# ScalarE stacks the row maxima itself, and the second scores follow 12 heads behind

## The reference, cut to what matters

```
x = x + attention0(layernorm(x), ctx, ctx)          # 16 heads of 16, no weights, softmax over 256 keys
x = x + moe(layernorm(x))                           # 64 experts, 8 of them for each token
x = x + attention1(layernorm(x), ctx) @ Wo.T        # projected q, k, v; causal
x = x + ffn(layernorm(x))                           # 16 blocks, 4 of them open for each token

scores = einsum('bqhd,bkhd->bhqk', q, k) * scale
attn   = softmax(scores)                            # exp(s - max over the keys) / sum
out    = einsum('bhqk,bkhd->bqhd', attn, v)
```

## Time and profile before

| | us |
|---|---|
| median of 3 runs | 1179.89 (1178.31 to 1189.08) |
| profiled execution, its own time | 1183.53 |
| its span | 1181.7 |
| busy: PE 934.0, PEld 627.6, DVE 614.7, ACT 360.8, POOL 535.2 | |
| DMA | 160.39 MB, mean 136 GB/s |

### The profile page before, as it was taken

The page is one execution under the profiler, slowest core; times in us unless marked ns, Lnnn a source line. Parts: engine busy times, 40 slices in busy tenths (PEclk is TensorE's granted clock), DMA queues, the critical chain, the costliest instruction groups (busy, mean ns, idle before and its releaser), DMA issues. The chain is left out here.

```text
span 1181.7 us, 22184 instructions
## 1 busy us (share of the span) xinstructions
PE 934.0 (79%) x5670; PEld 627.6 (53%) x5671; DVE 614.7 (52%) x1818; ACT 360.8 (31%) x884; POOL 535.2 (45%) x514
## 2 busy tenths in 40 slices
PE   1178778765499999999899999803788886799999
PEld 1035454454266666666666666502566664465665
DVE  6568988874144444444444444436878772333230
ACT  3426555613122222222222222111255564122211
POOL 4400776776476677676677667413253200000000
PEclk9999888988699999999999999955799999699999
DMA  6464534015455565555656666252877541100000
GB/s 221 156 161 126 112 87 101 24 32 170 139 188 187 160 206 186 179 183 176 194 186 207 206 199 205 78 218 70 251 193 213 147 105 30 58 9 10 18 18 19
DMA packets 78846, 160.39 MB, mean 136 GB/s; under 512 B 18448, under 2 KB 44048, under 8 KB 76480
## 3 DMA queue, kind: packets, MB, share of 16 engines
q1 hardware_dynamic: 59264, 112.23, 32.3%
q0 software_dynamic: 19520, 47.41, 13.0%
HBM read 118.09 MB, written 41.22 MB: 135 GB/s over the span
## 5 line engine op out<-in xcount | busy, mean ns | idle before, releaser
L1279 PE MATMUL ex_ps<-ex_w_gu,ex_rows_t 128*128 x640 | 263.1, 493 | 27.5 <-issue 17.0
L1248 POOL DMA_INDIRECT expert_outs<-ex_result,slot_places x160 | 157.4, 984 | 102.5 <-DVE ex_result L1391 101.6
L1243 POOL DMA_INDIRECT ex_rows<-moe_rows,slot_tokens x160 | 153.9, 962 | 57.7 <-issue 48.8
L881 POOL DMA_INDIRECT expert_lists<-rt_number,rt_idx x128 | 123.9, 968 | 105.8 <-DVE rt_idx L988 63.7
L1298 PE MATMUL ex_ps<-ex_w_down,ex_hidden_t 96*128 x640 | 166.8, 382 | 1.0 <-DVE ex_hidden_t L1383 1.0
L616 ACT ACTIVATE a_probs<-a_ps 128x512 f32<-128x512 f32 (+1 forms) x256 | 133.2, 541 | 96.3 <-PE a_ps L478 48.1
L1353 ACT ACTIVATE ex_act_g<-ex_ps 128x192 f32<-128x192 f32 x160 | 52.9, 330 | 353.3 <-PE ex_ps L1279 353.3
L461 PE MATMUL a_ps<-stacked_keys,a_qst 96*128 96x256 bf16 (+1 forms) x512 | 109.6, 287 | 56.4 <-DMA stacked_keys<-k_stack 26.7
L1279 PEld LDWEIGHTS ex_ps<-ex_w_gu,ex_rows_t 128*128 128x128 f32 x640 | 108.4, 192 | 43.2 <-issue 36.0
L1391 DVE TENSOR_SCALAR ex_result<-ex_ps,ex_rows 128x256 f32<-128x256 f32 x160 | 77.4, 484 | 93.5 <-PE ex_ps L1298 93.5
L1298 PEld LDWEIGHTS ex_ps<-ex_w_down,ex_hidden_t 96*128 96x128 f32 x640 | 108.3, 189 | 13.1 <-issue 2.4
(11 more groups left out here) (222 smaller groups left out, 1408.7 us busy)
## 6 DMA issues: line engine op xcount, KB each, us to landing
ex_w_gu<-in_w_gu_dram SPq DMA_DIRECT2D x64, 384.0 KB, 3.3
cb_gathered<-expert_outs SPq DMA_DIRECT2D x16, 1024.0 KB, 5.6
ex_w_down<-in_w_down_dram SPq DMA_DIRECT2D x64, 192.0 KB, 3.9
a_qst<-q_stack SPq DMA_DIRECT2D x32, 192.0 KB, 4.0
stacked_keys<-k_stack SPq DMA_DIRECT2D x32, 192.0 KB, 4.1
a_qst<-q_stack SPq DMA_DIRECT2D x32, 128.0 KB, 3.8
stacked_keys<-k_stack SPq DMA_DIRECT2D x32, 128.0 KB, 4.0
k_stack<-split_parts SPq DMA_DIRECT2D x8, 384.0 KB, 2.6
```

The source lines that it names most:

```text
L881: nc.gpsimd.indirect_dma_start(k.lists, bass.IndirectOffsetOnAxis(ap=self.idx[:, t, s:s + 1], axis=0), self.number[:, t, s:s + 1], None).t ...
L1243: nc.gpsimd.indirect_dma_start(rows[:, t % R, :], None, k.xn.rearrange("t p d -> (t p) d"), bass.IndirectOffsetOnAxis(ap=k.ids[:, begin + ...
L1248: nc.gpsimd.indirect_dma_start(k.outs, bass.IndirectOffsetOnAxis(ap=k.places[:, begin + t:begin + t + 1], axis=0), result[:, t % R], None) ...
L1279: last = pe.matmul(ps[:, 2 + j % 2, 0:2 * FF], rows_t[:, j % 2, c * P:(c + 1) * P], w_gu[:, bass.ds(ring, 1), c, :].rearrange("p a n -> p ...
```

## The change

In the first attention (`causal` false) and there alone:

- `qst` and the rows of `kst` that are used grow from 98 to 112. Rows 96 to 111 of the queries hold all 16 maxima rows (2 parts for each of 8 heads), the same in each head's slot; in the keys' stack, in head s's slot, rows 96+s and 104+s are ones and the other fourteen zeros.
- ACT writes these rows straight from PSUM into `qst` (`place_maxima`), in two copies of four heads' slots, 16x1024 each, at s = 1 and s = 2. `maxrows`, its copy and SP's two DMAs for each step are gone. `max_copied` counts both copies.
- POOL fills the one-hot rows at the start of the block with four `tensor_tensor` of 16x2048, ahead of its routing work. The fill with ones, which stood in `prepare`, now stands at the start of the second attention's block, ahead of `Combine`'s sums.
- `second(st, s)` puts the second scores, and all that hangs on them, 12 heads behind; the turn of the maxima moves from s = 4 to s = 1; `START` goes from 6 to 2.

```diff
-START = 6
+START = 2
...
+        def second(st, s):
+
+            at = s + (0 if causal else 4)
+            return (after(st, -LAG), at) if at < HSTEP else (after(st, 1 - LAG), at - HSTEP)
...
+                if causal:
+                    nc.gpsimd.memset(kst[ROWS:ROWS + mrows], 1.0).then_inc(keys_marked, 4)
+                    pool.wait_ge(keys_marked, 4)
+                else:
+                    heads = [k.ident_b[ROWS:ROWS + mrows, ROWS + part * HSTEP:ROWS + (part + 1) * HSTEP].unsqueeze(2).to_broadcast([mrows, HSTEP, SEQ])
+                             for part in range(2)]
+                    for u in range(4):
+                        nc.gpsimd.tensor_tensor(kst[ROWS:ROWS + mrows, u], heads[0], heads[1], ALU.add).then_inc(keys_marked, 1)
+                        pool.wait_ge(keys_marked, u + 1)
...
+                    if not causal and s % 4 == 0:
+                        pe.wait_ge(max_copied, 2 * h + 1 + s // 4)
...
-                        pe.wait_ge(max_copied, min(h + LAG, STEPS) if isinstance(h, int) else h + LAG)
+                        copies = 1 if causal else 2
+                        pe.wait_ge(max_copied, copies * min(h + LAG, STEPS) if isinstance(h, int) else copies * h + copies * LAG)
...
+                def place_maxima(st, g):
+                    h, u = number(st), st[1]
+                    act.wait_ge(max_turned, h + 1)
+                    nc.scalar.copy(qst[ROWS:ROWS + mrows, u, 4 * g:4 * g + 4, :],
+                                   max_t.unsqueeze(1).to_broadcast([mrows, 4, SEQ])).then_inc(max_copied, 1)
```

51 lines of the change are left out of this document (27 added, 24 removed).

## The result

| | before | changed |
|---|---|---|
| median, compared together (4 runs each) | 1184.49 us | 1197.30 us (1196.00 to 1202.48) |
| ratio, 95% interval | | 1.012 (1.0065 to 1.0175) |
| profiled execution, its span | 1183.53, 1181.7 us | 1196.41, 1194.5 us |
| mean granted clock of TensorE | 0.930 | 0.924 |

The change makes the kernel about 1.2% slower. The forecast was 1182.5 us, within 1175 to 1190: wrong. Of the 14.8 us between the forecast and 1197.3 us, 4.6 lie in the starting point (the forecast stood on a median of 1179.9 us of three runs, which with the fourth is 1184.5); the rest is the change, +12.8 us where +2.6 was forecast. The span grew by 12.8 us, and the block that was changed accounts for it: the scatter's last issue moved by 14.65 us.

A forecast was written before the change was run, and what follows sets the result against it. GpSimd's last scatter was taken to bound the kernel. Ramp -3.4, longer steps +2.4 and +2.0, then the sixth element's later places put its last issue at 295.3, +2.6 us: 1179.9 + 2.6 = 1182.5 us, range 1175 to 1190.

The forecast's parts named there:

- What bounds: First attention's block: GpSimd's last scatter ends it, at 292.72 us, and the kernel's time moves by as much.
- The ramp: Start of the attention: second scores at 72.7 us, the fifth head's 3.4 us earlier, bounds 0 to 3.7.
- The held cut: VectorE's two cuts at the start, beside GpSimd's additions: first held until 69.3 us, second slips through, 0 us in sum.
- the rival: Start of the attention: second cut held until 73.9 us, 2.8 us on top of the forecast, +5.4 in all; chance 0.10.
- Each step gets longer: Attention loop: outputs wait for ScalarE's copies; 0.6 us for each of four steps (+2.4), 0.25 for each of eight (+2.0).
- PE drops to half clock: Attention loop: PE's waits lower its granted clock; all five intervals at 23.3 us give +5.7 us; chance 0.12.
- near half clock: Attention loop wholly at half clock: an element takes 26.8 us, +23 us; chance 0.04.
- The sixth element binds: Scatter: sixth element's places come 21.9 us after the fifth's, at 231.1 us, so the last issue is at 295.3 us.
- the stall of the scatter: GpSimd's scatter: one stall of 4.2 us kept in the sum; a rival had it gone, 4.2 less, chance 0.05.
- Parts at nothing: Moved fill with ones (covered by 5.5 us in the second attention), SP's dropped DMAs and 112-row contraction: 0 us.

The follow-up runs named there:

- e14: Kernel with 12 heads' distance and DMA'd maxima (e2), order of the first scores' banks shifted by five heads: 1191.4 us, ratio 1.0042 to the kernel before.
- e1: Changed kernel with second scores 16 heads behind again and START 6, maxima still copied by ScalarE: 1185.8 us, ratio 1.0001 to the kernel before.
- e9: Kernel with 12 heads' distance and DMA'd maxima (e2), order of the first scores' banks shifted by four heads: 1189.3 us, ratio 1.0043 to the kernel before.
- e12: Kernel with 12 heads' distance and DMA'd maxima (e2), plus 12 useless transposes at head 7 of each step: 1190.0 us, ratio 1.0034 to the kernel before.
- e15: Changed kernel with only the filling added, the turn at head 7 done seven times over: 1200.2 us, ratio 1.0110 to the kernel before.
- e8: Kernel before with only the order of the first scores' three banks shifted by four heads: 1199.6 us, ratio 1.0130 to the kernel before.
- e2: Changed kernel with 12 heads kept, but maxima moved by one ScalarE copy and two DMAs as before: 1199.6 us, ratio 1.0134 to the kernel before.
- e16: e14 with the filling added, the turn at head 7 done seven times over: 1192.7 us, ratio 1.0065 to the kernel before.
- e17: e13 with head 7's second scores computed five times over in each step: 1196.1 us, ratio 1.0082 to the kernel before.
- e13: Kernel before with the order of the first scores' banks shifted by one head: 1183.0 us, ratio 0.9996 to the kernel before.
- e18: Changed kernel with banks shifted by five heads, first four heads' outputs one head later, and the filling at head 7: 1204.2 us, ratio 1.0149 to the kernel before.

## Why the prediction was wrong

- **What bounds: right.** The last scatter sets the end; it moved 14.65 us, the profiled execution 12.9; the difference was made up behind it.
- **The ramp: right in sign, too small.** Second scores at 71.23 us (forecast 72.7), fifth head's 5.3 us earlier (3.4). ScalarE's copies took 1.00 us (1.05), GpSimd's additions 3.60 us (4.5), and 1.7 us of the gain is the earlier load of step 1, which was not in the sum. (In the working of the copy, 1.55 us for 1792 numbers is 0.89 us for 1024, not 0.86; the sum does not use it.)
- **The held cut: right that it costs nothing, in part by luck.** The additions were shorter than forecast and ended at 68.79 us, not 73.9. The first cut was held, for 2.37 us, but by the fourth addition and not by the third. When the second cut came no addition was left to hold it, so the rival's +2.8 us had lost its condition, and this trace does not decide between the forecast and the rival. The Trainium skill, "GPSIMD Engine Reference", "Key points", names contention for VectorE's instructions with two SBUF inputs, and the second cut has two; no run here has it beside an addition. The held operations, this cut and the one in the earlier trace rows, have one SBUF input; whether they use both ports no row shows. That an operation with two SBUF inputs can slip through is shown elsewhere, in the second attention of the kernel before, where L87 starts between two of GpSimd's instructions, one that began at 800.91 us and took 4.49 us, and the next at 805.48 us:

```profile
801.08 4.34 DVE L85 SCALAR_TENSOR_TENSOR cb_newton<-cb_rstd 128x2 f32<-128x2 f32 x1
805.46 0.16 DVE L87 SCALAR_TENSOR_TENSOR cb_newton<-cb_moments,cb_newton 128x2 f32<-128x2 f32 x1
805.48 2.34 POOL L1504 TENSOR_TENSOR cb_gathered<-cb_gathered 128x1024 f32<-128x1024 f32 x1
```
- **"Each step gets longer": this step failed.** I took 0.6 us for each of the four steps before the first places and 0.25 us for each of the next eight. Measured: (119.31 - 118.72 + 5.3) / 4 = 1.47 us and (99.22 - 89.49) / 8 = 1.22 us. The mechanism that I put there is real (18 waits of 1.7 us; VectorE waited 12.5 us for first scores, against 2.5 before). But its price left out two things. The term carried START over as "the routing moves by the same four heads", as if nothing but second scores counted the heads: the banks of the first scores count them too. And each idle piece was priced at its own length, with the clock put off into a rival. That rival ("PE drops to half clock", all intervals at 23.3 us: +5.7; near half clock, +23) was right in kind, and its bound, a measurable loss once an element takes over 24.5 us, was just met: 122.59 / 5 = 24.5 us. It had 0.16.
- **The sixth element binds: right.** 23.37 us for its stretch, forecast 21.9; the stall of the scatter stayed (4.94 us). In e14, where the profile has the old pace up to the fifth element, the read-back came 2.2 us after the kernel before's. That is near the forecast's +2.6, but partly by luck: e14's profiled execution was one of its faster ones, and its median lies 6.6 us above the kernel before.
- **Parts at nothing: right.** The fill with ones is covered in the second attention, and e1 shows that the copies, the additions and the 112 rows are free 16 heads behind.

How the loss divides: taking away the narrow place is worth 3.1 us in the changed kernel and 8.2 to 10.3 us where no copies are in the way; taking away the copies is worth nothing with the narrow place and 4.9 us without. Both away, some 5 to 7 us above the kernel before remain (e9, e14; ratio 1.004, hardly told from 1). How much of the changed kernel's own loss goes through the clock is not shown: e12 shows it for the kernel with DMA'd rows, and in the changed kernel the same filling (e15) raised the clock and not the speed.

**Open:** what sets the clock from one element to the next. In e9 idle pieces of 1.88 and 2.24 us stand in stretches at 0.67, and pieces of 2.49 and 2.12 us in stretches at 0.92 and 1.00. In the changed kernel the third and fourth stretches have nearly the same idle pieces (2.04, 1.26 and 0.86 us; 2.06, 1.29 and 1.27 us), at clocks of 0.75 and 0.92. That shorter idle pieces helped is shown by e12; no length at which the clock falls is. Nor was the outputs' wait for bank 6 taken away while ScalarE's wide copies stayed 12 heads behind: the maxima and the outputs share that bank.

## What to carry to other kernels

When a schedule is shifted by some heads, list everything that counts heads modulo something (here a ring of three banks over eight heads), also code that the diff does not touch, and ask what lies ahead of its narrowest place now. Where two waits stand in for one another, taking away either shows nothing: take away both, and put one alone into the old kernel (e8 told more than the four runs before it). Price an idle piece of TensorE with the clock of the stretch behind it.

## What the runs showed of the hardware

- More work made the kernel faster: 12 useless transposes in a step's idle piece (3.08 down to 1.77 us) raised the granted clock of a stretch from between 0.74 and 0.86 to between 0.86 and 1.00 and saved 9.6 us (e12 against e2). Work of that kind gained nothing or cost 13 us where the pieces were already short (e16 against e14, e17 against e13).
- An element with 20 us of VectorE work took 21.2 to 22.6 us at a clock of 1.00 (e1, e12, e14), and 25.9 to 26.2 us at 0.67 (e9, e13). With ScalarE's copies 12 heads behind and the added transposes it took 23.5 to 24.0 us even at 1.00 (e18).
- Some of VectorE's operations on a few numbers, begun beside an addition of GpSimd, lasted until the addition had ended (2.37 us for a cast of 128x16, 4.34 us for an operation on 128x2), and the one right behind took 0.16 or 0.17 us.
- GpSimd's addition of 16x2048 bf16 took 3.60 us; ScalarE's copy of 16x1024 bf16 out of PSUM 1.00 us, of 16x256 0.36 us.
